# A six-layer decoder on one core: the eight-bit layer with its fine part and excess apart, the gated layer in 512 rows, and the grouped scores over four row groups

## The reference, cut to what matters

```
def _L0_ffn_ref(x, w_gate, w_up, w_down):            # 256 -> 1024 -> 256
    gate = einsum('bsd,hd->bsh', x, w_gate); up = einsum('bsd,hd->bsh', x, w_up)
    return einsum('bsh,dh->bsd', silu(gate) * up, w_down)

def _L1_xattn_ref(q, k, v, Wq, Wk, Wv, Wfc, bfc):     # 32 heads of 8, 8 groups of keys and values
    qh, kh, vh = heads of q @ Wq.T, k @ Wk.T, v @ Wv.T (kh, vh repeated 4 times)
    attn = softmax(einsum('bhqd,bhkd->bhqk', qh, kh) / sqrt(8))      # 64 keys per sequence
    return (attn @ vh) @ Wfc.T + bfc

def _L1_ffn_ref(input1, input2, scale, scale1):       # 256 x 256 weights
    q1 = (input1 * scale).astype(float8_e4m3fn); q2 = (input2 * scale1).astype(float8_e4m3fn)
    return einsum('bmk,kn->bmn', q1 / scale, q2 / scale1)
```

## Time and profile before

| | |
|---|---|
| three executions | 3243.87, 3261.5, 3262.87 us; median 3261.5 |
| profiled execution | 3276.46 us, span 3274.4 us, granted TensorE clock 0.905 in the mean |
| busy in the span | TensorE 2866.9 us (88%), weight loads 2497.6 (76%), VectorE 2082.4 (64%), ScalarE 1351.6 (41%), GpSimd 1318.2 (40%) |
| stages by the timeline | self-attention and cross-attention to about 1780 us; gated stage to 2106; quantised attention to 2747; grouped stage to 3109; eight-bit stage to the end |
| TensorE's busy tenths in 40 slices | 6999999995999999999996999679999995999821 |
| VectorE's | 5555555545888888888885444445657663666577 |

### The profile page before, as it was taken

The page is one execution under the profiler, slowest core; times in us unless marked ns, Lnnn a source line. Parts: engine busy times, 40 slices in busy tenths (PEclk is TensorE's granted clock), DMA queues, the critical chain, the costliest instruction groups (busy, mean ns, idle before and its releaser), DMA issues. The chain is left out here.

```text
span 3274.4 us, 65585 instructions
## 1 busy us (share of the span) xinstructions
PE 2866.9 (88%) x23120; PEld 2497.6 (76%) x23120; DVE 2082.4 (64%) x4286; ACT 1351.6 (41%) x3306; POOL 1318.2 (40%) x1661
## 2 busy tenths in 40 slices
PE   6999999995999999999996999679999995999821
PEld 6999999984888888888886999657777774788611
DVE  5555555545888888888885444445657663666577
ACT  2222222224656656656654333222323331666432
POOL 2111111113666666666663111124444543343334
PEclk9999999987999999999998999867779886999855
DMA  3000000002000000000001000100000000000000
GB/s 127 7 6 6 6 6 3 6 0 89 5 3 5 5 3 5 5 3 5 5 3 39 0 0 0 31 11 8 7 6 10 6 4 29 27 26 27 9 23 32
DMA packets 42636, 48.94 MB, mean 15 GB/s; under 512 B 4177, under 2 KB 33745, under 8 KB 42065
## 3 DMA queue, kind: packets, MB, share of 16 engines
q1 hardware_dynamic: 42576, 48.16, 4.5%
HBM read 35.57 MB, written 4.19 MB: 12 GB/s over the span
## 5 line engine op out<-in xcount | busy, mean ns | idle before, releaser
L124 POOL TENSOR_SCALAR sh_rstd<-sh_meanvar 128x2 f32<-128x2 f32 (+1 forms) x112 | 24.9, 222 | 810.0 <-DVE sh_meanvar L116 624.2
L1077 POOL TENSOR_TENSOR b_rows<-b_rows,b_swapped 128x512 f32<-128x512 f32 x160 | 204.1, 1284 | 133.2 <-DVE b_swapped L864 133.2
L1018 ACT ACTIVATE b_probs<-bank,b_shift,b_q_scale 128x128 f32<-128x128 f32 x512 | 228.1, 458 | 71.6 <-DVE b_shift L895 71.6
L504 POOL TENSOR_TENSOR a_probs<-a_probs,a_rs 128x512 f32<-128x512 f32 x64 | 66.8, 1044 | 325.0 <-DVE a_rs L403 317.8
L46 PE MATMUL bank<-a_xT,a_wq 128*128 128x256 f32 x512 | 154.2, 301 | 39.7 <-DVE a_xT L370 39.7
L1124 POOL TENSOR_TENSOR b_probs<-b_probs,b_rs 128x512 f32<-128x512 f32 x128 | 133.4, 1042 | 112.3 <-DVE b_rs L915 108.9
L1087 POOL TENSOR_TENSOR b_rms<-b_rms,sh_minus_half 128x8 f32<-128x8 f32 (+1 forms) x128 | 169.9, 1327 | 10.7
L2544 ACT ACTIVATE d_probs<-d_probs 128x512 f32<-128x512 f32 x128 | 78.4, 629 | 231.5 <-DVE d_probs L2441 231.5
L872 DVE TENSOR_REDUCE b_ss<-b_squares 128x4 f32<-128x512 f32 x192 | 125.2, 680 | 60.0 <-ACT b_squares L993 60.0
L1795 DVE TENSOR_REDUCE e_mx<-bank 128x8 f32<-128x512 f32 x128 | 86.2, 684 | 119.5 <-PE bank L1701 119.5
L1271 DVE TENSOR_TENSOR c_h<-c_silu,bank 128x256 f32<-128x256 f32 x128 | 53.9, 421 | 160.8 <-ACT c_silu L1308 160.8
(11 more groups left out here) (343 smaller groups left out, 9909.1 us busy)
## 6 DMA issues: line engine op xcount, KB each, us to landing
a_xT_in<-in_xT SPq DMA_DIRECT2D x16, 256.0 KB, 2.7
sh_x<-in_x SPq DMA_DIRECT2D x1, 4096.0 KB, 25.0
b_ctx_in<-in_ctxT SPq DMA_DIRECT2D x32, 128.0 KB, 2.0
d_x_in<-sh_x SPq DMA_DIRECT2D x16, 256.0 KB, 2.3
e_x_in<-sh_x SPq DMA_DIRECT2D x16, 256.0 KB, 2.3
e_cT<-in_ctxT SPq DMA_DIRECT2D x32, 128.0 KB, 2.5
out<-sh_x SPq DMA_DIRECT2D x16, 256.0 KB, 2.1
a_qT<-in_L_attn_Wq SPq DMA_DIRECT2D x1, 2048.0 KB, 8.5
```

Of the source, the lines that this page charges most:

```text
L1018: op = act.activation(probs[:, g % 2, keys], bS[:, keys], ACT.Exp, bias=shift[:, g % 2, a:a + 1], scale=q_scale[:, g, a // 2, a % 2:a % 2 ...
L1077: pool.tensor_tensor(rows[:, unit, :], rows[:, unit, :], swapped[:, half, :], ALU.add).then_inc(added[unit], 1)
```

## The change

**Eight-bit stage.** The quantiser class goes. ScalarE writes `coarse`, half the scaled value cast to eight bits, `scaled`, and from `coarse` by Relu the amount `under` below -224; VectorE writes `fine`, the scaled value clamped to 224 and cast to eight bits in one operation, `over`, the amount above 224 from `coarse`, and `excess` as their difference in eight bits. TensorE multiplies `fine` and `excess` apart by the weights (bf16) into one bank, 8 matmuls of 256 columns per turn. x is transposed from `sh.x` itself. The residual is one operation of 512 columns that unscales too. GpSimd does only the two-column operations; ScalarE makes the normalised x by Identity with scale and bias. All buffers are doubled, the 16 turns are unrolled, and the waits are on constants.

**Gated stage.** Turns of 512 rows (8 of them). Gate and up have two banks each of 512 columns, with a semaphore each; x is turned into two banks; the four tiles of y share two banks. `WideRows` holds four tiles for residual and normalisation. `gate_up(front, 0)` and `(front, 1)` each move one `down` earlier.

**Grouped stage.** `scores` does all four row groups in one call, so there are two calls per turn. All four engines have new orders, with `four_deep`: values are projected one turn later than keys and queries, output projection and moments two. `three_deep` goes.

```diff
+class WideRows:
+    def __init__(self, sh, sb, n):
+        self.x, self.minus_half, self.passed_dve, self.passed_pool = sh.x, sh.minus_half, sh.passed_dve, sh.passed_pool
+        self.res, self.stats, self.meanvar = sb("res", [128, n, D]), sb("stats", [128, n, 6]), sb("meanvar", [128, n, 2])
+        self.rstd, self.shift = sb("rstd", [128, n]), sb("shift", [128, n])
 def gated_mlp_block(nc, sh):
...
-        bA, bT, bY = sh.bank[0:3], sh.bank[3], sh.bank[6:8]
+        bG, bU, bT = sh.bank[0:2], sh.bank[2:4], sh.bank[4:6]
+        bY = [sh.bank[6 + r // 2][:, r % 2 * D:(r % 2 + 1) * D] for r in range(NR)]     # NR = 4, N = 512
...
+            def gate_up(i, j):
+                pe.wait_ge(h_ready, nth(i, J, max(j - 1, 0)))
+                if j == 0:
+                    pe.wait_ge(x_low, nth(i, C, C))
+                for w, bank, ready in ((wg, bG, g_ready), (wu, bU, u_ready)):
                     for c in range(C):
+                        last = product(pe, bank[j % 2][:, :], parts(lambda a: w[:, a, c, j * 128:(j + 1) * 128]),
                                        parts(lambda a: xT[:, a, c, :]), start=(c == 0), stop=(c == C - 1))
+                    last.then_inc(ready, 1)
...
             def turn(cur, front):
                 for j in range(J - 2):
                     gate_up(cur, j + 2)
                     down(cur, j)
                     if j == 2 and front is not None:
                         turn_x(front)
+                if front is not None:
+                    gate_up(front, 0)
                 down(cur, J - 2)
                 if front is not None:
-                    gate_up(front, 0)
+                    gate_up(front, 1)
                 down(cur, J - 1)
-                if front is not None:
-                    gate_up(front, 1)
...
             def take_x(i):
-                act.wait_ge(turned, nth(i, 1, 1))
-                act.wait_ge(gu_ready, nth(i, J, 0))
+                act.wait_ge(u_ready, nth(i, J, 0))
+                for c in range(C):
+                    act.wait_ge(turned, nth(i, C, c + 1))
+                    act.copy(xT[:, 0, c], bT[c][:, :]).then_inc(x_high, 1)
...
 def fp8_matmul_block(nc, sh):
+    FINE, TOP = 224.0, 112.0
...
+            def turn_rows(i):
+                free(pe, scaled_ready, i)
...
+                        last = pe.transpose(bT[i % 2][:, c * 256 + r * 128:c * 256 + (r + 1) * 128],
+                                            sh.x[:, 2 * i + r, c * 128:(c + 1) * 128], sh.ident[:, :])
+                last.then_inc(turned, 1)
+            def multiply(i):
+                pe.wait_ge(excess_ready, i + 1)
+                free(pe, res_ready, i)
+                for r in range(2):
+                    for k, part in enumerate((fine, excess)):
                         for c in range(C):
+                            last = pe.matmul(bY[i % 2][:, r * D:(r + 1) * D], part[:, i % 2, c * 256 + r * 128:c * 256 + (r + 1) * 128],
+                                             w[:, c * D:(c + 1) * D], start=(k == 0 and c == 0), stop=(k == 1 and c == C - 1))
+                last.then_inc(y_ready, 1)
...
+            def scale_rows(i):
+                act.wait_ge(turned, i + 1)
+                free(act, over_ready, i)
+                act.activation(coarse[:, i % 2, :], bT[i % 2][:, :], ACT.Copy, scale=halves[:, 0:1], saturate=False).then_inc(coarse_ready, 1)
+                act.activation(scaled[:, i % 2, :], bT[i % 2][:, :], ACT.Copy, scale=scales[:, 0:1]).then_inc(scaled_ready, 1)
+            def below(i):
+                act.wait_ge(coarse_ready, i + 1)
+                free(act, excess_ready, i)
+                act.activation(under[:, i % 2, :], coarse[:, i % 2, :], ACT.Relu, bias=edge[:, 0:1], scale=-2.0).then_inc(under_ready, 1)
+            def normalise_rows(i):
+                act.wait_ge(shift_ready, i + 1)
+                for r in range(2):
+                    act.activation(sh.x[:, 2 * i + r, :], res[:, i % 2, r, :], ACT.Identity,
+                                   scale=rstd[:, i % 2, r:r + 1], bias=shift[:, i % 2, r:r + 1]).then_inc(normed, 1)
...
+            for i in range(n_turns + 2):     # ScalarE
+                scale_rows(i + 1); normalise_rows(i - 2); below(i + 1)        # each where its turn exists
...
+            def round_fine(i):
+                dve.wait_ge(scaled_ready, i + 1)
+                free(dve, y_ready, i)
...
+                dve.tensor_scalar(fine[:, i % 2, :], scaled[:, i % 2, :], FINE, -FINE, ALU.min, ALU.max, saturate=False).then_inc(fine_ready, 1)
+                dve.tensor_scalar(over[:, i % 2, :], coarse[:, i % 2, :], TOP, 2.0, ALU.max, ALU.mult).then_inc(over_ready, 1)
+            def take_excess(i):
+                dve.wait_ge(under_ready, i + 1)
+                dve.wait_ge(over_ready, i + 1)
...
+                dve.scalar_tensor_tensor(out=excess[:, i % 2, :], in0=over[:, i % 2, :], scalar=-2.0 * TOP, in1=under[:, i % 2, :],
+                                         op0=ALU.add, op1=ALU.subtract, saturate=False).then_inc(excess_ready, 1)
...
+            for i in range(1, n_turns + 1):  # VectorE
+                round_fine(i); take_excess(i)                                 # while i < n_turns
+                residual(i - 1)
...
 def grouped_cross_attention_block(nc, sh):
...
                 for c in range(C):
-                    for n in (2 * half, 2 * half + 1):
+                    for n in range(4):
...
+            def turn(new, mid, old, oldest):     # TensorE
+                project_v(mid); turn_probs(old, 0, 7, True); weigh(oldest, 7); scores(old, 1, 1, False)
+                turn_probs(old, 1, 0, False); turn_att(oldest, mid); weigh(old, 0); turn_probs(old, 2, 1, False)
+                turn_x(new, oldest); weigh(old, 1); turn_probs(old, 3, 2, False); project_out(oldest, mid)
+                turn_probs(old, 4, 3, False); weigh(old, 2); weigh(old, 3); scores(mid, 0, 6, True)
+                turn_probs(old, 5, 4, False); weigh(old, 4); turn_probs(old, 6, 5, False); project_k(new)
+                weigh(old, 5); project_q(new, oldest); turn_probs(old, 7, 6, False); weigh(old, 6)
+            def turn(new, mid, old, oldest):     # VectorE
+                moments(oldest); take_att(old, 1, 7)
+                maximum(mid, 7); maximum(mid, 5); maximum(mid, 4); shift(mid, 4); shift(mid, 5); maximum(mid, 6); shift(mid, 7); shift(mid, 6)
+                residual(old); take_att(mid, 0, 3)
+                maximum(new, 3); maximum(new, 2); maximum(new, 0); maximum(new, 1); shift(new, 0); shift(new, 3); shift(new, 2); shift(new, 1)
+            def turn(new, mid, old, oldest):     # ScalarE
+                exponent(old, 3); take_pT(old, 2, 0, False); exponent(old, 4); take_x(new); take_pT(old, 3, 1, False)
+                exponent(old, 5); take_pT(old, 4, 2, False); exponent(old, 6); take_pT(old, 5, 3, False); take_k(new)
+                exponent(old, 7); take_pT(old, 6, 4, False); take_q(new); exponent(mid, 0); take_pT(old, 7, 5, False)
+                exponent(mid, 1); exponent(mid, 2); take_pT(mid, 0, 6, True); take_v(new, old); take_pT(mid, 1, 7, True); take_att(old)
+            def turn(new, mid, old, oldest):     # GpSimd
+                spread_k(new); normalise(oldest); add_bias(old)
```

More of the change, by code:

```diff
@@ L1234, in down @@
                 if j == 0:
[L1235 to L1240, removed]
+                    pe.wait_ge(res_ready, nth(i, NR, 0))
+                for r in range(NR):
+                    last = product(pe, bY[r], parts(lambda a: hT[:, a, j, r * 128:(r + 1) * 128]), parts(lambda a: wd[:, a, j, :]),
+                                   start=(j == 0 and r % 2 == 0), stop=(j == J - 1 and r % 2 == 1))
+                    if j == J - 1 and r % 2 == 1:
+                        last.then_inc(y_ready, 2)
             def turn(cur, front):
@@ L1440, in fp8_matmul_block @@
-        n_turns = sh.turns // 2
+        edge = sb("edge", [128, 1])
+        scaled = sb("scaled", [128, 3, 512])
+        coarse = sb("coarse", [128, 3, 512], FP8)
+        over = sb("over", [128, 3, 512], BF16)
+        under = sb("under", [128, 3, 512], BF16)
+        fine = sb("fine", [128, 3, 512], FP8)
+        excess = sb("excess", [128, 3, 512], FP8)
+        res = sb("res", [128, 2, 2, D])
+        stats = sb("stats", [128, 2, 6])
+        meanvar = sb("meanvar", [128, 2, 2, 2])
+        spread = sb("spread", [128, 2, 2])
@@ L1459, in _ @@
+            for i in range(n_turns):
+                sp.wait_ge(normed, 2 * (i + 1))
+                sp.dma_start(t["out"].rearrange("(n p) d -> p n d", p=128)[:, 2 * i:2 * i + 2, :],
+                             sh.x[:, 2 * i:2 * i + 2, :]).then_inc(written, 16)
             sp.wait_ge(written, 16 * n_turns)
@@ new lines, in residual @@
+            def residual(i):
+                dve.wait_ge(y_ready, i + 1)
+                free(dve, normed, i, 2)
+                hold(dve, sh.passed_dve)
```

(18 more changed lines are left out.)

436 lines of the change are left out of this document (191 added, 245 removed).

## The result

The changed kernel takes 3153.2 us (median of 4 runs, 3143.9 to 3164.6) where the kernel before, on the same chip, takes 3262.2 (3243.9 to 3266.9). The ratio is 0.9683, 95% interval [0.9645, 0.9722]: faster by 3.2%. The forecast was 3145, its range 3115 to 3185.

The account below looks back on a forecast made before the run. TensorE was taken to bound the gated and grouped stages, VectorE the eight-bit stage. Terms of -90, -22 and -4 sum to -116 us: 3276.5 becomes 3160 profiled, and the median 3261.5 becomes 3145; range 3115 to 3185.

Parts of the forecast that it names:

- Eight-bit stage, -90: Eight-bit stage: VectorE's turn falls from 8.73 to 3.60 us, the stage from 165.4 to 75 us.
- 11.3 + 57.6 + 6: Eight-bit stage's forecast length: head 11.3 us, 16 turns of 3.60 making 57.6, tail 6; together 75 us.
- the first rival: Eight-bit stage: ScalarE binds the turn, for instance through table loads, 5.2 us a turn; 26 us back, 3171; chance 0.10.
- The cover of `under`: Eight-bit stage: ScalarE's step is ready 3.2 us after the moments of i-2, before VectorE comes after 4.5 us.
- Grouped stage, -22: Grouped stage: merged scores and new order cut the turn from 19.73 to 18.5 us; 22 us less, between 8 and 30.
- the stalls: Grouped stage: TensorE loses about 0.3 us a turn at copies of transposed probabilities and 0.2 around `take_v`.
- 13 of 18 us: Grouped stage: ScalarE has 13 us of work per turn in a fixed order and 18 to do it in.
- the second rival: Grouped stage: scores are quicker but TensorE waits for ScalarE's copies, turn stays 19.7; 22 us back, 3167; chance 0.13.
- Gated stage, -4: Gated stage: 512-column matmuls save 10 us, waits and two more end tiles take some back; between -10 and +6 us.
- The two waits: Gated stage, per 512 rows: 1.4 us lost before the next turn's first gate, 1.7 before the second gated product.
- 10/8 - 0.3 = 0.95: Gated stage, per 512 rows: 10 us of matmul saving over 8 turns, less 0.3 us more waiting per turn.
- more than forecast: Grouped stage keeps TensorE fed (8 us more) and the gated stage's boundary waits vanish (20 us): 3117; chance 0.08.

Follow-up runs that it names:

- f_only: The kernel before with only the eight-bit stage of the changed kernel: 3168.2 us, ratio 0.9715 to the kernel before.
- e_only: The kernel before with only the grouped stage of the changed kernel: 3248.0 us, ratio 0.9945 to the kernel before.

## Why the prediction was right

The forecast was 116 us less. Against the medians it is 109, and by stages 92 (eight-bit), about 14 (grouped) and 0.5 (gated). The large term was right with its mechanism; the two small ones both gave less than forecast.

*Eight-bit stage, -90: right, -92.* The turn was put at 3.60 and is 3.52. The stage is 13.4 us to the first residual (3072.5 to 3085.86), 51.4 for 15 intervals (the first and last are shorter) and 8.2 from the last residual to the end; I had 11.3 + 57.6 + 6, with 16 whole turns and too short a head and tail, two errors that partly cancel. (The head's own terms add up to 10.6, not 11.3.) `over` is at the low end, 0.42. The Trainium skill (DVE: opcode table, instruction layouts, handler registers and perf-mode slots, "Perf-mode slots") has an eight-bit one-source operation reach a mode of two elements per cycle; the trace agrees in so far as `over` takes as long as the 32-bit one-source rows. There is no table load in the stage and the turn is short, so the first rival is out.

The cover of `under` was misjudged: I put 3.2 us from the moments of i-2 to the excess, against 4.5 until VectorE comes. Measured from the end of the moments, 3112.22, to the excess of the second turn after (3113.27 + 3.51 = 3116.78) it is 4.56, and VectorE would be there after 4.27. The term most mis-sized is GpSimd's, 2.6 us to `shift` instead of 1.7. `rstd` takes 1.25 us beside `excess` and 0.71 in the last turn, when VectorE is idle, and the first `spread` 0.57 and 0.23. From `shift` to the excess it is 1.9 us instead of 1.5. I had seen that GpSimd's wide passes stretch VectorE's operations; that VectorE stretches GpSimd's small ones I had not.

*Grouped stage, -22: about -14, since the steady turn was forecast too short.* Cut into the first stretch, twelve steady turns, and the rest, the kernel before and then the changed one:

```profile
2746.50:2822.70 76.20, 56.01 (x586) 42.88 (x588) 30.40 (x53) 30.68 (x70) 17.11 (x16) 0.78 0.14 45
2822.70:3059.50 236.80, 236.80 (x3178) 190.63 (x3175) 157.52 (x300) 152.56 (x336) 97.70 (x97) 1.00 0.08 26
3059.50:3109.10 49.60, 39.65 (x474) 31.19 (x470) 22.56 (x47) 20.66 (x42) 17.00 (x20) 0.79 0.00 1
```

```profile
2729.60:2805.70 76.10, 54.67 (x669) 43.45 (x670) 32.38 (x58) 34.31 (x84) 20.80 (x18) 0.84 0.16 49
2805.70:3036.50 230.80, 219.80 (x3171) 179.93 (x3170) 157.15 (x301) 146.69 (x337) 98.09 (x97) 1.00 0.08 25
3036.50:3072.50 36.00, 26.26 (x389) 20.69 (x388) 20.14 (x43) 15.76 (x29) 13.33 (x19) 0.93 0.01 2
```

The steady turns gave 6.0 us, not the 15 that a turn of 18.5 would have given in twelve. Fill and drain together gave 13.7 (125.8 to 112.1 us). They can only be read together, since the changed kernel does 83 matmuls more in its first stretch and 85 fewer in its last: the work of four turns is divided between them in another way. Part of the 13.7 is the clock. In f_only, which has the grouped code of before, they take 120.0 us, the last stretch 44.9 of them at granted clock 0.94; in e_only, which has the new code, 115.4. So about 8 us there are the change's, with 5 to 14 as the extremes. The forecast had 5 for the scores of these four turns, 2 for the partial turns, and 0 to 5 against it. Which of its terms was right there isn't shown. The step that failed is the stalls: 0.3 and 0.2 us at the copies were forecast, and in the changed kernel TensorE was busy 219.8 of 230.8 us where it had been 236.8 of 236.8. TensorE's own work was nearly as forecast: with the stall behind `take_v` shortened, the turn is 18.53. I judged ScalarE by its total (13 of 18 us) and not by its densest stretch, 7.45 us without a pause. The turn of 19.24 is past the 19.2 that I had named as making the forecast wrong; by that measure the second rival, "the grouped turn stays 19.7", was nearer in the steady part than the forecast.

*Gated stage, -4: within its range, -0.5.* The two waits came where they were put, 1.4 and 1.7 us forecast, 1.21 and 1.70 measured. With 37.76 us for 512 rows against twice 19.0 the turn gains 0.2, where 10/8 - 0.3 = 0.95 was forecast. So the missing 0.7 us isn't in these two waits; no run places it. The 0.7 us before `down` in the kernel before are two waits, 0.55 and 0.18. Removing the waits gives 19 us, as the rival "more than forecast" had it (20), but it takes an order that the change doesn't have.

*The offset.* Between two executions of the same code, quantised attention differs by more than the gated and grouped errors together; see below.

## What to carry to other kernels

Judge an engine's cover by the densest stretch between two of its deadlines, not by its total per turn. When wide elementwise work shares the turn between VectorE and GpSimd, count the stretching both ways, and move the wide part to ScalarE. When tiles grow from 256 to 512 rows, write out the order around the turn's boundary again: with the fewer, longer waits there the wider matmuls gained nothing, and a reordering of one engine gave 19 us.

## What the runs showed of the hardware

Quantised attention, the same code in every kernel, took 612 to 640 us in fourteen profiles. Its turns in the changed kernel, cut at GpSimd's last operation:

```profile
2309.80:2339.50 29.70, 27.75 (x306) 21.90 (x305) 22.95 (x49) 11.29 (x25) 16.63 (x28) 1.00 0.02 9
2339.50:2374.60 35.10, 33.38 (x307) 26.59 (x306) 22.77 (x49) 11.31 (x25) 16.61 (x29) 0.81 0.02 7
...
2538.90:2578.70 39.80, 38.09 (x320) 30.72 (x318) 23.74 (x51) 12.24 (x26) 16.64 (x29) 0.75 0.02 7
```

The same turn is 29.7 us at granted clock 1.00 (2.4 GHz), 35.1 at 0.81 and about 37.5 at 0.75, mixtures with the 1.2 GHz level (the 39.8 us hold 320 matmuls where a turn has 306, and the window behind them has 294 in 35.1 us), with VectorE's and GpSimd's busy time nearly unchanged. Each execution has its own sequence: the one with 612.3 us alternates 29.7 and 35.1 from its second turn nearly to its end, the one with 640.0 has windows of 38 to 40 three times. It is of the size by which one kernel's runs lie apart (before, 3243.9 to 3266.9); what sets the sequence stays open.

The eight-bit stage of before, with four matmuls in 8.7 us, had the clock at 0.50 throughout; with eight in 3.5 us the mean of the stage is 0.69, and 0.64 in f_only, where the turn is 3.52 too. The forecast had allowed for 0.50 and needed nothing from it, since TensorE waits there for `excess` in any case.
